# A decoder layer on one core: the prologue by batch halves, decay and beta by token, the softplus series on POOL, and a new order for the first head

## The reference

```python
q = _dwconv_silu(x @ Wq.T, conv_q).reshape(B, L, H, DH)
k = _dwconv_silu(x @ Wk.T, conv_k).reshape(B, T, H, DH)
v = _dwconv_silu(x @ Wv.T, conv_v).reshape(B, T, H, DH)
beta = jax.nn.sigmoid(x @ Wb.T).reshape(B, T, H) * 2.0
g = -jnp.exp(A_log) * jax.nn.softplus(x @ Wa.T + dt_bias)
...
state = state * jnp.exp(g_t)[..., None, None]
corr = jnp.einsum('bhk,bhkv->bhv', k_t, state)
v_new = (v_t - corr) * b_t[..., None]
state = state + jnp.einsum('bhk,bhv->bhkv', k_t, v_new)
```

## Time and profile before

| | |
|---|---|
| runs | 618.31, 618.94, 618.95 us; median 618.94 |
| profiled execution | 617.76 us, of them 616.0 in the span |
| busy, share of the span | PE 91%, DVE 75%, ACT 58%, POOL 4% |
| mean granted TensorE clock | 0.961 |
| by the chain that ended last | PE 72%, DVE 16%, ACT 8%, issue 2%, DMA 1% |

### The profile page before, as it was taken

How to read it: one execution, slowest core, us unless ns; L and a number is a source line. 1 busy time by engine, 2 the same in 40 slices (tenths; PEclk the granted TensorE clock), 3 DMA queues, 4 the chain that set the end, 5 groups by cost and what they waited for, 6 DMA issues and landing times.

```text
span 616.0 us, 15291 instructions
## 1 busy us (share of the span) xinstructions
PE 558.9 (91%) x6463; PEld 376.4 (61%) x6463; DVE 460.0 (75%) x1091; ACT 356.0 (58%) x555; POOL 26.3 (4%) x36
## 2 busy tenths in 40 slices
PE   3769879999999999999999999999997979758997
PEld 2325336577757675766576667657766857646646
DVE  6577898877979797978788878887795612589663
ACT  0748394588459655946684768458842322277451
POOL 3011000100010001000100100010000000100000
PEclk9979999999999999999999999999997978967999
DMA  5000203101110121021002101110101140000002
GB/s 162 1 0 2 70 9 71 28 1 27 56 27 1 27 58 25 10 65 14 22 14 65 11 20 22 59 28 2 27 11 29 24 150 3 1 0 2 0 1 68
DMA packets 49699, 18.62 MB, mean 30 GB/s; under 512 B 39100, under 2 KB 48352, under 8 KB 49632
## 3 DMA queue, kind: packets, MB, share of 16 engines
q1 hardware_dynamic: 49632, 17.66, 12.1%
HBM read 14.49 MB, written 3.15 MB: 29 GB/s over the span
## 4 chain that ended last, share of the span: by engine, by line
PE 72%; DVE 16%; ACT 8%; issue 2%; DMA 1%; SPq 0%; ACTq 0%; DVEq 0%
PE bank L1167 16%; DVE acc L790 8%; PE bank L1214 6%; PE bank L1340 4%; PE bank L1344 4%; PE bank L1129 4%; PE bank L1431 3%; PE bank L1233 3%; PE bank L1299 3%; PE bank L1356 3%; PE bank L1217 3%; PE bank L1350 3%; PE bank L1352 2%; PE bank L1354 2%; PE bank L1211 2%
## 5 line engine op out<-in xcount | busy, mean ns | idle before, releaser
L790 DVE SCALAR_TENSOR_TENSOR acc<-bank,cw,acc 128x508 f32<-128x508 f32 (+2 forms) x240 | 176.4, 739 | 41.9 <-ACT acc L508 37.6
L1167 PE MATMUL bank<-xnT,wq 128*128 128x512 f32 x320 | 154.8, 610 | 16.2 <-DVE acc L790 15.7
L1167 PEld LDWEIGHTS bank<-xnT,wq 128*128 128x128 f32 x320 | 56.4, 191 | 75.9 <-issue 45.3
L508 ACT ACTIVATE acc<-bank,cw 128x512 f32<-128x512 f32 x80 | 55.5, 694 | 46.9 <-PE bank L1167 46.2
L1214 PE MATMUL bank<-kq 128*128 128x384 f32 x128 | 50.7, 499 | 0.2
L523 ACT ACTIVATE vT<-acc 128x512 f32<-128x512 f32 x32 | 21.3, 673 | 46.1 <-DVE acc L790 46.0
L821 DVE SCALAR_TENSOR_TENSOR AM<-bank,rb,DT 128x384 f32<-128x384 f32 x64 | 37.5, 606 | 1.8 <-PE bank L1214 1.5
L554 ACT ACTIVATE T<-bank 64x512 f32<-64x512 f32 x16 | 9.5, 592 | 44.9 <-PE bank L1233 34.6
L883 DVE SCALAR_TENSOR_TENSOR xres<-bank,f,xres 128x256 f32<-128x256 f32 x64 | 26.9, 478 | 10.3 <-PE bank L1344 10.0
L573 ACT ACTIVATE Yd<-Yc 32x512 f32<-32x512 f32 x32 | 20.1, 628 | 21.3 <-DVE Xc L870 21.0
L523 ACT ACTIVATE kq<-acc 128x512 f32<-128x512 f32 x48 | 31.4, 658 | 1.2 <-DVE acc L790 0.9
(11 more groups left out here) (242 smaller groups left out, 1083.8 us busy)
## 6 DMA issues: line engine op xcount, KB each, us to landing
wq<-in_w_qkv SPq DMA_DIRECT2D x8, 640.0 KB, 4.1
blocks<-AM SPq DMA_DIRECT2D x128, 8.0 KB, 1.6
xres<-in_x SPq DMA_DIRECT2D x2, 512.0 KB, 4.6
Yl<-in_y_init SPq DMA_DIRECT2D x8, 128.0 KB, 2.6
Bl<-blocks SPq DMA_DIRECT2D x8, 128.0 KB, 2.0
wg<-in_w_gate SPq DMA_DIRECT2D x8, 128.0 KB, 2.1
solved<-Yl SPq DMA_DIRECT2D x8, 128.0 KB, 2.4
Yc<-solved SPq DMA_DIRECT2D x64, 16.0 KB, 2.0
```

What stands on the lines that cost most here:

```text
L508: a(acc[:, u % RING, :, :], bank[6 + u % 2][:, :].rearrange("p (b l) -> p b l", b=4), ACT.Copy, scale=cw[:, t, 3:4]).then_inc(s_tap.next(f ...
L790: stt(w, ps[:, :, 0:L - s], cw[:, t, 3 - s:4 - s], w, ALU.mult, ALU.add).then_inc(s_cv.next(f"u{u}_{s}"), 1)
L1167: ins = mm(bank[6 + u % 2][:, :], wq[:, cc, t, :], xnT[:, cc, 512 * half:512 * half + 512], start=cc == 0, stop=cc == KC - 1)
```

## The change

The statistics, roots, normalizations, transposes and copies go by halves of 4 batches (`statistics`, `variance`, `normalized`, `turn_half`, `turned_half`), and the copies of a half are split between ScalarE and VectorE. TensorE's first projection stands ahead of the second half's transposes. Decay and beta are made with `xnT` as the stationary operand and `wba` moving, 16 products of 24 columns that come out with tokens in partitions. The doubling to steps is a product with a constant 0/1 matrix `twice`. The softplus series stands on POOL, apart from one reciprocal on VectorE; beta too. The orders of the first phase are new, and SP loads head 1's `wq` after the last projection of head 0.

```diff
-FIRST_SCALAR_ORDER = ("+0 +1 -0 +2 -1 +3 +4 -2 q0 +5 -3 -4 +6 -5 dt0 +7 q1 dt1 +8 dt2 cs +9 nr -6 -7 -8 -9").split()
+FIRST_SCALAR_ORDER = ("+0 +1 +2 +3 -0 -1 -2 q0 +4 +5 -3 -4 +6 -5 q1 +7 dt0 +8 dt1 +9 dt2 cs nr -6 -7 -8 -9").split()
...
             start_solve()
+            sp.wait_ge(s_pro.sem, s_pro.at(f"u{NU - 1}", 0))
+            load_projection(1)
             sp.wait_ge(s_cv.sem, s_cv.at(f"u{NU - 1}_3", 0))
-            load_projection(1)
             load_convolution(1)
...
-            pool.wait_ge(s_preD.sem, s_preD.at("gl"))
...
+            pool.wait_ge(s_preA.sem, s_preA.at("raw"))
+            pk(gt(zz, raw[:, :, :], rep(dtb[:, :].rearrange("p (o h) -> p o h", o=1), 1, B), ALU.add))
+            gs(po, zz, 0.0, None, ALU.min)
+            pk(gs(raw[:, :, :], zz, 0.0, None, ALU.max))
+            gt(ez, raw[:, :, :], po, ALU.subtract).then_inc(s_preG.next("gz"), 1)
+            pool.wait_ge(s_preA.sem, s_preA.at("gexp"))
+            gs(ra, ez, 2.0, None, ALU.add).then_inc(s_preG.next("rs"), 1)
+            pool.wait_ge(s_preD.sem, s_preD.at("rr"))
+            pk(gt(ra, ra, ez, ALU.mult))
+            pk(gt(r2, ra, ra, ALU.mult))
+            pk(gs(po, r2, 2.0 / 17, 2.0 / 15, ALU.mult, ALU.add))
+            for k in (13, 11, 9, 7, 5, 3, 1):
+                pk(gt(po, po, r2, ALU.mult))
+                pk(gs(po, po, 2.0 / k, None, ALU.add))
+            pk(gt(po, po, ra, ALU.mult))
+            pk(gt(po, po, raw[:, :, :], ALU.add))
+            pool.wait_ge(s_preA.sem, s_preA.at("aexp"))
+            pk(gt(po, po, rep(al[:, :].rearrange("p (o h) -> p o h", o=1), 1, B), ALU.mult))
+            gs(gl[:, :, :], po, -1.0, None, ALU.mult).then_inc(s_preG.next("gl"), 1)
...
             decay_rows(0)
+            pool.wait_ge(s_preA.sem, s_preA.at("steps"))
+            pk(gt(beta[:, :, :], bsig[:, :, 1, :], bsig[:, :, 0, :], ALU.subtract))
+            pk(gs(beta[:, :, :], beta[:, :, :], cm[:, 0:1], None, ALU.mult))
+            pk(gt(beta[:, :, :], beta[:, :, :], bsig[:, :, 0, :], ALU.add))
+            gs(beta[:, :, :], beta[:, :, :], 2.0, None, ALU.mult).then_inc(s_preG.next("bparity"), 1)
...
+            def decays():
+
+                act.wait_ge(s_preP.sem, s_preP.at("gates"))
+                a(raw[:, :, :], bank[5][:, 0:24 * B].rearrange("p (b h) -> p b h", b=B)[:, :, 16:24], ACT.Copy).then_inc(s_preA.next("raw"), 1)
+                act.wait_ge(s_preG.sem, s_preG.at("gz"))
+                a(sm[1][:, :, :], sm[1][:, :, :], ACT.Exp, scale=-1.0).then_inc(s_preA.next("gexp"), 1)
...
+            statistics(0)
+            variance(0)
+            statistics(1)
+            normalized(0)
+            variance(1)
+            turned_half(0)
+            normalized(1)
+            turned_half(1)
...
+                dve.wait_ge(s_preG.sem, s_preG.at("rs"))
+                v.reciprocal(sm[2][:, :, :], sm[2][:, :, :]).then_inc(s_preD.next("rr"), 1)
...
+            def decays():
+
+                turned(1)
                 for b in range(B):
+                    for cc in range(KC):
+                        ins = mm(bank[5][:, 24 * b:24 * b + 24], xnT[:, cc, L * b:L * b + L], wba[:, cc, :], start=cc == 0, stop=cc == KC - 1)
+                ins.then_inc(s_preP.next("gates"), 1)
                 pe.wait_ge(s_preG.sem, s_preG.at("zero"))
+
+            def steps_of_delta():
+
+                pe.wait_ge(s_preG.sem, s_preG.at("twice"))
+                pe.wait_ge(s_preA.sem, s_preA.at("sig"))
+                for half in range(NH):
+                    ins = mm(bank[3][:, P * half:P * half + P], twice[:, half, :], tokb[:, :, :].rearrange("p b n -> p (b n)"), start=True, stop=True)
+                ins.then_inc(s_preP.next("steps"), 1)
+
+            turn_half(0)
+            turned(0)
```

More of the change, by code:

```diff
@@ L171, in build @@
         sm = [sb(f"sm{i}", [P, B, H]) for i in range(5)]
+        raw = sb("raw", [P, B, H])
+        tokb = sb("tokb", [P, B, 16])
+        twice = sb("twice", [P, NH, P])
         al = sb("al", [P, H])
@@ L302, in build @@
         s_ch = sem("vector_chain")
-        PRE_D = (["var"] + ["xn" + str(b) for b in range(B)] + [f"xt{i}" for i in range(4)] + ["bparity", "gz", "gl"])
+        PRE_D = (["var0"] + [f"xn{b}" for b in range(4)] + ["var1", "x0"] + [f"xn{b}" for b in range(4, B)] + ["x1", "rr"])
         s_preD = Signal(sem("vector_prologue"), PRE_D)
-        s_preA = Signal(sem("scalar_prologue"), ["sdev", "ba0", "ba1", "sig", "gexp", "aexp", "eu"])
-        s_preP = Signal(sem("tensor_prologue"), [f"xt{i}" for i in range(4)] + ["ba0", "ba1", "ba"])
-        s_preG = Signal(sem("pool_prologue"), ["zero", "bounds"])
+        s_preA = Signal(sem("scalar_prologue"), ["sdev0", "sdev1", "x0", "x1", "raw", "gexp", "aexp", "eu", "sig", "steps"])
+        s_preP = Signal(sem("tensor_prologue"), ["t0", "t1", "gates", "steps"])
+        s_preG = Signal(sem("pool_prologue"), ["zero", "twice", "bounds", "gz", "rs", "gl", "bparity"])
+        s_pch = sem("pool_chain")
         UH = [(t, f) for f in range(2) for t in range(HT)]
@@ L445, in _ @@
             g.memset(sel[:, 31:32], 1.0).then_inc(s_preG.next("zero"), 1)
+            pool.wait_ge(s_first.sem, s_first.at("w_ba"))
+            for half in range(NH):
+                each = ident[:, 64 * half:64 * half + 64].rearrange("p (l o) -> p l o", o=1)
+                i = g.tensor_copy(twice[:, half, :].rearrange("p (l o) -> p l o", o=NH), rep(each, 2, NH))
+            i.then_inc(s_preG.next("twice"), 1)
             pool.wait_ge(s_ld.sem, 16 * N_LD)
@@ L597, in phase @@
                             tap(int(step[1:]), h + 1)
-                            if step == "+1" and not (old or now):
-                                gates()
+                            if h == -1 and step == "+0":
+                                turned_half(1)
+                            elif h == -1 and step == "+1":
+                                decays()
+                            elif h == -1 and step == "+2":
+                                constants()
+                            elif h == -1 and step == "+3":
+                                steps_of_delta()
+                            elif h == -1 and step == "+4":
+                                each_step()
                     elif step[0] == "-":
@@ L916, in phase @@
                             conv(*steps.pop(0), h + 1)
-                            if len(steps) == 3 * NU - 6 and not (old or now):
+                            if len(steps) == 3 * NU - 6 and h == -1:
                                 gates()
@@ L1130, in _, with turn_half @@
             pe.wait_ge(s_first.sem, s_first.at("w_ba"))
[L1131 to L1134 removed]
+            def turn_half(f):
+                for b in range(4 * f, 4 * f + 4):
                     pe.wait_ge(s_preD.sem, s_preD.at(f"xn{b}"))
[L1136 to L1142 removed]
@@ L1144, in gates @@
-            def gates():
-                pe.wait_ge(s_preA.sem, s_preA.at("ba1"))
-                for ch in range(CH):
-                    half, b = ch // B, ch % B
-                    t0 = (NH * b + half) * P
-                    nc.tensor.transpose(bank[3][:, 16 * ch:16 * ch + 16], stepT[:, t0:t0 + P], ident[0:16, 0:16])
+                    for cc in range(KC):
+                        c = P * (b % 4)
+                        ins = tr(bank[2 * f + cc][:, c:c + P], xn[:, b, P * cc:P * cc + P])
@@ L1365, in phase @@
                             project(int(step), h + 1)
-                            if step == "1" and not (old or now):
-                                gates()
+                            if h == -1 and step == "0":
+                                turn_half(1)
+                            elif h == -1 and step == "1":
+                                decays()
+                            elif h == -1 and step == "4":
+                                steps_of_delta()
                     elif step in prep.names or step == "ca":
```

119 lines of the change are left out of this document (51 added, 68 removed).

## The result

| | before | after |
|---|---|---|
| runs, us | 618.31 to 620.04 (5) | 613.99 to 616.24 (5) |
| median | 618.95 | 615.77 |
| ratio | | 0.9938, 95% interval 0.9925 to 0.995 |
| profiled execution | 617.76, span 616.0 | 616.24, span 614.5 |
| granted clock | 0.961 | 0.956 |

The account below looks back on a forecast made before the run. TensorE is busy 69.52 of 70 us in the middle, so only an earlier start counts: head 1's first projection from 66.21 to 58.4, 7.8 us, carried through from 618.94 to 611.1; range 608.4 to 615.3.

Parts of the forecast that it names:

- Halves: Start of the kernel: first projection at 12.15 instead of 17.86, units 0 and 1 convolved from 17.0, 3.6 us gained.
- The cold start: TensorE's first projection: clock up at about 14 us, projection ends at 15.1; never cold would give 1.2 us back.
- Gates: Gate products on TensorE: 16 products taking 3.8 us, 17.8 to 21.6, with projection 2 right behind.
- Series: Softplus series on POOL: 0.43 and 0.35 us per linked instruction, `Gb` done at 34.9, 2.2 us of cover for `dt0`.
- Units 2 and 3: VectorE's convolutions of these units: from 24.7 instead of 32.94, 8.2 us gained, the largest step.
- Tap 4 and the gap: ScalarE ahead of unit 4: tap 4 at 32.3, unit 4 at 33.0, 6.6 us gained; TensorE idles 4.4 us.
- the rival with its 0.17: Clock falls in TensorE's new gap ahead of projection 6: gain 6.0, result 612.9; chance 0.17.
- 6: Units 4 to 9: 13.5 us of convolutions plus waits for taps, `ss` at about 49.0 instead of 54.49.
- 7: Key products and values ahead of head 1: 9.4 to 9.5 us, so TensorE reaches head 1 at 58.4.
- wq: Load of head 1's `wq` goes out about 45, lands at 49; by itself worth little, 0.28 us idle before.
- Nothing in the later phases changes, so I carry 7.8 through: Everything behind head 1's first projection: the 7.8 us gained there reaches the end whole.
- The rule weighed: Table loads on ScalarE: skill's drain of about 1.38 us per switch, tap 4 2.8 later, result 613.9; chance 0.01.

Follow-up runs that it names:

- Experiment 5: Changed kernel with tap 4 ahead of the SiLUs, plus five 128x512 zero products ahead of TensorE's first transposes: 627.04 us, ratio to before 1.0162.
- 1: Changed kernel plus 38 small unused products on TensorE between projections 5 and 6, to hold the clock: 614.94 us, ratio to before 0.9927.
- 3: Changed kernel with the softplus series back on VectorE, beta staying on POOL: 616.08 us, ratio to before 0.9941.
- 11: Changed kernel with tap 4 moved ahead and 64 tiny products at TensorE's start, a whole block (256 instructions): 610.99 us, ratio to before 0.9859.
- 4: Changed kernel with the 16 gate products in two groups, the first ahead of projection 1: 614.32 us, ratio to before 0.991.
- 15: Changed kernel plus 62 tiny products at TensorE's start (248 instructions, 8 short of a block): 613.72 us, ratio to before 0.9925.
- 9: Changed kernel plus 64 tiny products at TensorE's start, a whole block (256 instructions): 615.01 us, ratio to before 0.9919.
- 6: Changed kernel with tap 4 moved ahead and twelve one-column products (24 instructions) behind projection 5: 624.70 us, ratio to before 1.0099.
- 13: Changed kernel with tap 4 ahead, twelve one-column products behind projection 5 and 58 tiny products at TensorE's start: 611.73 us, ratio to before 0.9874.
- 17: Changed kernel with tap 4 moved ahead and 62 tiny products at TensorE's start (248 instructions): 608.38 us, ratio to before 0.9821.
- 18: Changed kernel with tap 4 moved ahead and 64 tiny products at TensorE's start, a control run (256 instructions): 611.38 us, ratio to before 0.9879.
- 16: Kernel before the change plus 2 tiny products at TensorE's start (8 instructions): 618.76 us, ratio to before 0.9998.
- 12: Changed kernel with tap 4 moved ahead and 124 tiny products at TensorE's start (496 instructions): 614.16 us, ratio to before 0.992.
- 10: Kernel before the change plus 64 tiny products at TensorE's start (shift +248 against the changed kernel): 618.98 us, ratio to before 0.9994.

## Why the prediction was wrong

By its own steps:

1. *Halves.* First projection 11.93 for 12.15, its end 15.3 for 15.1, first convolution 16.82 for 17.0. The cold start went as taken. Experiment 5 prices it at 1.8 us for the projection, where the prediction had 1.2, and 0.9 for the transposes. The granted clock doesn't show this start: it reads 1.00 from 9 to 15 us, and only the durations (1.94 against 1.04 for the same eight transposes) tell.
2. *Gates.* 3.65 us for 3.8. What it missed: the clock can fall behind these thin products (four of 15 profiled executions of the changed kernel and its variants), and then projections 2 and 3 take 5.38 (the changed kernel, experiments 1, 3 and 11). That is 0.9 us by tap 4, a term that the sum had at nothing. In these four executions the first projection had taken 3.37 to 3.54 us, in the ten others with a cold start 3.75, without exception: the instructions are the same, so the fall goes with when the clock came up at the start. Why, no run shows.
3. *Series.* Linked instructions on POOL started 0.40 to 0.47 apart (two pairs 0.33 and 0.38), `Gb` ended at 35.37 for 34.9, and `dt0` began at 39.99, covered. Right, but by experiment 3 the move isn't worth anything that can be measured in this order.
4. *Units 2 and 3*: 25.37 for 24.7.
5. *Tap 4 and the gap.* **The first failure.** "Whether that lowers the clock no row says" was true, but the rival with its 0.17 was the likelier case: in five profiled executions with a gap of 3.7 us or more the clock fell in four (changed, 3, 4, 15, not in 9), in nine with a gap of 1.5 us or less ahead of projection 6 in none (in 11, with 2.21 us, it did). Its price was also too small: 1.8 us counted projection 6 alone, but `dt0` behind it was slow as well, so that from projection 6 to projection 7 it was 5.69 us instead of 2.90 in experiment 9. So the failed term is the gap's clock loss, 0 in the sum and 2.8 us measured. Tap 4 came 1 us late (33.36 for 32.3); with the clock up it is at 32.49, so 0.9 of that is the fall at 22 us.
6. *and* 7. With the clock up the walk holds: experiment 9 has projection 6 at 35.54 (forecast 35.35), `ss` at 48.96 (49.0) and the door at 58.59 (58.4). So of the 3.9 us missing at the door 3.7 are the clock, 2.8 behind the gap and 0.9 behind the gate products.
8. *wq* waits for nothing now, as said.

**The second failure** is the sentence behind the sum: "Nothing in the later phases changes, so I carry 7.8 through". TensorE's list got 8 instructions longer ahead of them, which moved every border between blocks of instructions by 8, and from 290 to 462 us the profiled execution lost 3.9 us against the kernel before. Experiments 6 and 13 show that the place in a block decides (12 us by 24 instructions, taken back by 232 more), 17 and 18 that 8 are enough to be seen in the total, 15 and 16 in the traces alone. Part of the loss is given back by the end (-0.4 at 462, 1.5 at the end), 1.4 us of it between 500 and 520 us, where the clock was down for 13.7 us before (499.31 to 512.97) and for 10.2 after (499.48 to 509.72); why that differs wasn't tried. This second failure is the smaller one: the door of the profiled execution was 3.9 us earlier and the medians differ by 3.2, so of the 4.6 us that were missing 3.9 were missing at the door. All kernels wait for instructions in the last head (2.7 to 4.1 us at once) whatever the shift.

The rule weighed falls too: the load of the table at 28.93 took 1.28 us, and the SiLU stood at 30.22, 0.01 later. By the Trainium skill ("ScalarE: Activation LUTs", "What ACT_TABLE_LOAD costs") it would have been 1.4 later; the trace shows no such drain.

Open stays why the clock falls in one execution and not in the next with the same instructions (9 and the changed kernel), and so how often the changed kernel pays for it. That the rise of the clock at the start goes with the fall at 22 us is all that the traces give.

## What to carry to other kernels

Where a start is rearranged and the rest is a full plateau, read the gaps that the new order leaves on TensorE as a cost in clock, with all that runs behind them, and move the one instruction that ends the gap, before anything larger is moved. Count the instructions that an edit adds ahead of a stretch of tiny products: if such a stretch uses a block faster than the next one lands, its place in the block is worth microseconds per pass, and a few products of nothing in an idle place at the start can set it right (15 and 17), if they are not so many that they hold up the start (12). And measure a small edit with and without a neutral shift before believing what its total says about the edit.

## What the hardware showed

- Adding 24 instructions of 0.44 us in sum to TensorE's list cost 12 us; adding 256 (9 to 11) cost nothing.
- The waits for instructions up to 475 us, all runs taken together, ended 2.24 to 3.08 us after the start of a 16-KB packet whose transfer took 0.88 to 1.44 us.
- The clock fell while TensorE was busy without a gap, behind 3.65 us of products with 24 columns, in 4 of 15 executions.
- On POOL instructions on 64 columns took 0.32 us with two inputs and 0.37 to 0.38 with one (one of each kind was shorter, 0.29 and 0.24), so one input isn't cheaper.
- The first projection of the kernel before and its variants began between 17.51 and 18.87 us in five profiled executions. This spread of 1.36 us is more than many edits here are worth, so doors of that kernel are best counted from it.
